# Attention and expert layers in eight tiles: two interleaved fronts and a third special step at the start

## The reference

```python
q, k = sigmoid(x Wq + bq), sigmoid(x Wk + bk); v = x Wv + bv
sink_in  = n / sum_d((q+e) * (cumsum(k)+e));  src_out = n / sum_d((k+e) * (cumsum(q)+e))
cons_sink = sum_d((q+e) * (cumsum(k*src_out)+e)) / n
cons_src  = exp(clip(sum_d((k+e) * (cumsum(q*sink_in)+e)) / n, -1, 1))
vs = v * cons_src / cumsum(cons_src) * n
a  = (q*sink_in/n) . cumsum(k outer vs) * sigmoid(cons_sink)
h  = layernorm(x + a Wo + bo); z = layernorm(h + gelu(h W1 + b1) W2 + b2)
x2 = layernorm(x + z)
y  = layernorm(x2 + sum_e gate_e * (relu(x2 wi + bi + x2 A_e B_e) wo + bo))
```

## Time and profile before

| what | us |
|---|---|
| median of 3 runs (lowest, highest) | 417.70 (417.43, 417.96) |
| the profiled execution's own time | 417.23 |
| its span, first to last instruction | 415.4 |
| busy: TensorE, VectorE, GpSimd, ScalarE | 374.7, 329.4, 252.0, 216.7 |
| mean granted clock of TensorE | 0.991 of full |

### The profile page before, as it was taken

The page is one execution under the profiler, slowest core; times in us unless marked ns, Lnnn a source line. Parts: engine busy times, 40 slices in busy tenths (PEclk is TensorE's granted clock), DMA queues, the critical chain, the costliest instruction groups (busy, mean ns, idle before and its releaser), DMA issues. The chain is left out here.

```text
span 415.4 us, 6622 instructions
## 1 busy us (share of the span) xinstructions
PE 374.7 (90%) x2082; PEld 261.7 (63%) x2082; DVE 329.4 (79%) x787; ACT 216.7 (52%) x399; POOL 252.0 (61%) x431
## 2 busy tenths in 40 slices
PE   8897799788998999989998999899999997799991
PEld 3555556475756875677657774778478755675551
DVE  3659966699599988999799979997899889732632
ACT  2240326327853586538852785279635864175441
POOL 2017245995289828975598449963898279836211
PEclk9999999899999999999999999999999999999997
DMA  8236006400180007300560028001800072000000
GB/s 260 113 75 154 1 2 156 123 2 0 39 216 2 0 2 188 93 0 0 122 158 2 1 71 211 2 0 29 211 17 0 2 178 51 0 1 28 14 13 25
DMA packets 19859, 26.59 MB, mean 64 GB/s; under 512 B 1648, under 2 KB 9968, under 8 KB 19824
## 3 DMA queue, kind: packets, MB, share of 16 engines
q1 hardware_dynamic: 19680, 25.96, 24.5%
q10 hardware_dynamic: 144, 0.21, 0.2%
HBM read 7.29 MB, written 2.10 MB: 23 GB/s over the span
## 5 line engine op out<-in xcount | busy, mean ns | idle before, releaser
L848 POOL TENSOR_TENSOR prod<-cum_kv,q_fac 128x512 f32<-128x512 f32 x64 | 92.3, 1452 | 31.6 <-DVE cum_kv L1054 24.7
L404 PEld LDWEIGHTS pO<-s_wor,prod 128*128 128x128 f32 x512 | 62.9, 193 | 34.1 <-POOL prod L848 21.5
L404 PE MATMUL pO<-s_wor,prod 128*128 128x128 f32 x512 | 70.3, 284 | 14.1 <-POOL prod L848 13.9
L1048 DVE TENSOR_TENSOR kv<-k,vb 128x512 f32<-128x512 f32 x64 | 52.9, 826 | 6.8 <-DMA vb<-vs 6.8
L835 POOL TENSOR_TENSOR var_eps<-mv,s_con 128x4 f32<-128x4 f32 x32 | 9.5, 296 | 59.4 <-DVE mv L1076 59.4
L1054 DVE TENSOR_TENSOR_SCAN cum_kv<-p_ones,cum_kv,kv 128x512 f32<-128x512 f32 x32 | 40.5, 1275 | 0.6
L1054 DVE TENSOR_TENSOR_SCAN cum_kv<-p_ones,kv 128x512 f32<-128x512 f32 x32 | 38.6, 1215 | 0.5
L657 ACT ACTIVATE v<-pA,s_att 128x512 f32<-128x512 f32 x7 | 4.8, 687 | 62.4 <-PE pA L340 62.4
L754 ACT ACTIVATE relu<-pG,s_att 128x512 f32<-128x512 f32 x28 | 19.1, 684 | 27.4 <-PE pG L490 27.4
L508 PEld LDWEIGHTS pY<-s_moe,gel 128*128 128x128 f32 x256 | 30.7, 192 | 3.7 <-issue 1.9
L508 PE MATMUL pY<-s_moe,gel 128*128 128x128 f32 x256 | 32.6, 277 | 0.0
(11 more groups left out here) (164 smaller groups left out, 806.2 us busy)
## 6 DMA issues: line engine op xcount, KB each, us to landing
vb<-vs SPq DMA_DIRECT2D x64, 256.0 KB, 4.6
xT<-x_t SPq DMA_DIRECT2D x8, 256.0 KB, 4.1
xt<-x SPq DMA_DIRECT2D x8, 256.0 KB, 5.1
out<-y SPq DMA_DIRECT2D x8, 256.0 KB, 2.3
s_moe<-moe_w SPq DMA_DIRECT2D x1, 836.0 KB, 10.1
s_wor<-wo_rep SPq DMA_DIRECT2D x1, 512.0 KB, 7.9
s_ffn<-ffn_w SPq DMA_DIRECT2D x1, 512.0 KB, 8.6
s_con<-consts SPq DMA_DIRECT2D x1, 502.0 KB, 4.5
```

Source lines behind the costliest of these rows:

```text
L404: mm = pe.matmul(pO3[:, s, :], prod[:, m % 4, s * P:(s + 1) * P], s_wor[:, m, :], start=False, stop=(m == DH - 1), skip_group_check=True)
L848: pool.tensor_tensor(prod[:, m % 4, :], cum_kv[t.par][:, m, :], q_fac[t.par][:, :], ALU.mult).then_inc(prod_ready, 1)
L1048: dve.tensor_tensor(kv[:, m % 3, :], k[t.par][:, :], vb[:, m, :], ALU.mult).then_inc(kv_ready, 1)
```

## The change

The step after the second gets a program of its own. Tile 1's q and k are projected in the opening, into two other banks (pG[1] and pM), and its first running sums and denominators are done there between those of tile 0. The second step keeps tile 0's outer products and the rest of tile 1's front, with no FFN; its VectorE program alternates running sums with other operations. The third step has tile 0's FFN and part of its experts, tile 1's outer products and FFN, and tile 2's front and first outer products. The general step starts at tile 2, and leaves out what the third step did for it. Several helpers get a further wait, since the buffers rden, rden_n, rden_x, kq, qk and vb are now written in another order. The diff, cut to its core (q_times_cum_k and the other sums get waits like those shown; head_sums and project_k follow the banks):

```diff
--- before
+++ after
+def q_bank(t):
+    return pG[1] if t.n == 1 else pA
+
+def k_bank(t):
+    return pM if t.n == 1 else pB
...
+def p_den(t):
+    return k_bank(t)[:, SUMS_AT:SUMS_AT + 2 * HW]
...
     def spread_vs(t, m):
         sp.wait_ge(vs_ready, t.n + 1)
+        wait(sp, kv_ready, DH * (t.n - 1) + m + 1)
...
+    load_xT(Tile(2))
...
     def project_q(t):
-        wait(pe, qfac_ready, t.n)
-        pe.matmul(pA[:, :], att("wq"), xT[t.par][:, :], start=True, stop=True).then_inc(q_proj, 1)
+        if t.n > 1:
+            pe.wait_ge(qfac_ready, t.n)
+        pe.matmul(q_bank(t)[:, :], att("wq"), xT[t.par][:, :], start=True, stop=True).then_inc(q_proj, 1)
...
     def project_v(t):
-        if t.n > 0:
+        if t.n == 1:
+            pe.wait_ge(qfac_ready, t.n)
+        elif t.n > 1:
...
     def denominators_T(t, i):
...
+            wait(pe, vs_ready, t.n)
...
@@ TensorE @@
     def opening(a):
+        b = a.plus(1)
         project_q(a); project_k(a); project_v(a)
-        keep_busy(1)
         pe.matmul(pO[:, :], onesrow[:, 0:P], onesrow[:, :], start=True, stop=True).then_inc(po_written, 1)
+        project_q(b); project_k(b)
         head_sums(a, 0, True); head_sums(a, 0, False)
         keep_busy(2)
         denominators_T(a, 0); denominators_T(a, 1)
         keep_busy(3)
         head_sums(a, 1, True); head_sums(a, 1, False)
         keep_busy(1)
+        head_sums(b, 0, True)
         cumulate_e(a)
-        keep_busy(2)
+        head_sums(b, 0, False)
+        keep_busy(1)
         compensation_T(a); factor_T(a)
+        keep_busy(3)
+        project_v(b)
+        denominators_T(b, 0); denominators_T(b, 1)
         constant_row()
-        project_q(a.plus(1)); project_k(a.plus(1))
-        keep_busy(4)
         pe.wait_ge(y_free[0], 16)
         reduce_out(a, 0)
     def second_step(b):
         a = b.plus(1)
-        keep_busy(2)
-        for m in range(1, 5):
-            reduce_out(b, m)
-        head_sums(a, 0, True); head_sums(a, 0, False); project_v(a)
         keep_busy(1)
-        reduce_out(b, 5)
-        denominators_T(a, 0); denominators_T(a, 1)
+        reduce_out(b, 1)
         keep_busy(1)
-        reduce_out(b, 6)
+        reduce_out(b, 2)
+        keep_busy(1)
         head_sums(a, 1, True)
         keep_busy(1)
         head_sums(a, 1, False)
         keep_busy(1)
+        reduce_out(b, 3)
+        keep_busy(1)
+        reduce_out(b, 4)
+        keep_busy(2)
+        reduce_out(b, 5)
+        cumulate_e(a)
+        keep_busy(1)
+        reduce_out(b, 6)
+        compensation_T(a); factor_T(a)
+        keep_busy(1)
         reduce_out(b, 7)
+    def third_step(c):
+        b, a = c.plus(1), c.plus(2)
+        project_q(a); project_k(a)
+        keep_busy(1)
+        project_v(a)
         keep_busy(2)
+        pe.wait_ge(y_free[1], 16)
+        h_T(c); hidden(c, 0); hidden(c, 1)
+        head_sums(a, 0, True); head_sums(a, 0, False)
+        hidden(c, 2); hidden(c, 3); ffn_out(c, 0)
+        reduce_out(b, 0)
+        ffn_out(c, 1)
+        reduce_out(b, 1)
+        ffn_out(c, 2)
+        denominators_T(a, 0); denominators_T(a, 1)
+        ffn_out(c, 3)
+        reduce_out(b, 2)
+        keep_busy(1, pM)
+        reduce_out(b, 3)
+        keep_busy(2, pM)
+        reduce_out(b, 4)
+        keep_busy(1, pM)
+        head_sums(a, 1, True)
+        keep_busy(1, pM)
+        head_sums(a, 1, False)
+        keep_busy(1, pM)
+        reduce_out(b, 5)
+        keep_busy(1, pM)
+        reduce_out(b, 6)
+        keep_busy(1, pM)
         cumulate_e(a)
-        keep_busy(2)
-        h_T(b); compensation_T(a); factor_T(a)
-        for f in range(FC):
-            hidden(b, f)
+        reduce_out(b, 7)
+        keep_busy(1, pM)
+        compensation_T(a); factor_T(a)
+        pe.wait_ge(cmoe_ready, 1)
+        x2_T(c)
+        keep_busy(1, pG[1])
+        logits(c)
+        h_T(b); hidden(b, 0); hidden(b, 1)
+        lora_in(c)
+        hidden(b, 2); hidden(b, 3)
         for f in range(FC):
             ffn_out(b, f)
-        keep_busy(3, pM)
+        u_T(c, True)
+        inter_base(c, 0); inter_base(c, 1)
+        u_T(c, False)
+        inter1(c, 0); inter1(c, 1)
         reduce_out(a, 0)
+        inter2(c, 0); inter2(c, 1)
...
     def step(s):
-        if s.n == 1:
-                    pe.wait_ge(y_free[1], 16)
-                    pe.wait_ge(cmoe_ready, 1)
...
-    run_steps(step, first=1, end=TILES)
+    third_step(Tile(0))
+    run_steps(step, first=2, end=TILES)
...
@@ ScalarE @@
     def spread_denominators(t, i):
+        wait(act, (facT_ready, compT_ready)[i], t.n)
...
-        q_out(a); k_out(a)
-        spread_denominators(a, 0); spread_denominators(a, 1); v_out(a)
+        b = a.plus(1)
+        q_out(a); k_out(a); v_out(a)
+        q_out(b); k_out(b)
+        spread_denominators(a, 0); spread_denominators(a, 1)
         source_exp(a); alloc_tanh(a); allocation(a)
         spread_scale(a, False); spread_scale(a, True)
-        q_out(a.plus(1)); k_out(a.plus(1))
         seed_x(a)
+        spread_denominators(b, 0); spread_denominators(b, 1); v_out(b)
     def second_step(b):
         a = b.plus(1)
-        v_out(a); spread_denominators(a, 0); spread_denominators(a, 1)
         source_exp(a); alloc_tanh(a); allocation(a)
-        normalise(b, 0)
         spread_scale(a, False); spread_scale(a, True)
-        h_out(b)
+    def third_step(c):
+        b, a = c.plus(1), c.plus(2)
+        q_out(a); k_out(a)
+        normalise(c, 0); v_out(a); seed_x(b); h_out(c)
+        gelu(c, 0); gelu(c, 1)
+        seed_h(c)
+        gelu(c, 2); gelu(c, 3)
+        spread_denominators(a, 0); spread_denominators(a, 1)
+        normalise(c, 1)
+        source_exp(a); alloc_tanh(a); allocation(a)
+        spread_scale(a, False); spread_scale(a, True)
+        normalise(c, 2)
+        x2T_out(c); normalise(b, 0); gate_exp(c); h_out(b)
         gelu(b, 0); gelu(b, 1)
-        seed_h(b)
-        gelu(b, 2); gelu(b, 3)
+        seed_h(b); gelu(b, 2); gelu(b, 3)
         seed_x(a)
+        u1T_out(c)
+        act.wait_ge(cmoe_ready, 1)
+        udT_out(c); relu(c, 0); relu(c, 1)
+        gated_constant(c)
         normalise(b, 1)
...
@@ GpSimd @@
     def second_step(b):
-        for m in range(1, DH):
+        for m in range(1, 4):
             product(b, m)
-        inverse_std(b, 0); e_normal(a); scaled_h(b); h_residual(b); attention_input(a)
-        shifted_x(b); inverse_std(b, 1); product(a, 0); scaled_n2(b)
+        attention_input(a)
+        for m in range(4, 6):
+            product(b, m)
+        e_normal(a)
+        product(b, 6); product(b, 7)
+    def third_step(c):
+        b, a = c.plus(1), c.plus(2)
+        inverse_std(c, 0); scaled_h(c); h_residual(c)
+        product(b, 0); product(b, 1); shifted_x(c); product(b, 2); product(b, 3)
+        attention_input(a)
+        product(b, 4); inverse_std(c, 1); scaled_n2(c)
+        product(b, 5); outer_residual(c)
+        product(b, 6); e_normal(a); product(b, 7); shifted_x(b)
+        inverse_std(c, 2); inverse_std(b, 0); scaled_h(b); h_residual(b)
+        product(a, 0); product(a, 1)
+        inverse_std(b, 1); product(a, 2); scaled_n2(b)
     def step(s):
-        if B: product(b, 1); product(b, 2)
+        if B and b.n > 2: product(b, 1); product(b, 2)
...
@@ VectorE @@
     def k_times_cum_q(t, pair):
+        wait(dve, (consp_ready, den_ready)[pair], 2 * (t.n + pair))
...
     def inverse_denominators(t):
+        wait(dve, qscale_ready, t.n)
...
     def normal_denominators(t):
+        wait(dve, rdenx_ready, 2 * t.n)
...
     def cumulate_sink(t):
+        if t.par == 1:
+            dve.wait_ge(cumqs_ready, t.n)
...
+    def opening(a):
+        b = a.plus(1)
+        cumulate_q(a); cumulate_k(a); k_times_cum_q(a, 0); q_times_cum_k(a, 0)
+        inverse_denominators(a); normal_denominators(a)
+        cumulate_q(b)
+        sink(a); cumulate_sink(a); source(a); k_times_cum_q(a, 1); cumulate_source(a); q_times_cum_k(a, 1)
+        cumulate_k(b)
+        k_times_cum_q(b, 0)
+        conserved(a); clip_source(a)
+        q_times_cum_k(b, 0)
+        prefix_e(a)
+        inverse_cum_e(a); source_factor(a); sink_factor(a)
+        inverse_denominators(b)
+        values(a); query_factor(a)
+        normal_denominators(b)
+        outer_product(a, 0); cumulate_kv(a, 0); outer_product(a, 1)
     def second_step(b):
         a = b.plus(1)
+        cumulate_kv(b, 1); outer_product(b, 2)
+        sink(a); cumulate_sink(a); k_times_cum_q(a, 1)
+        cumulate_kv(b, 2); outer_product(b, 3)
+        source(a); cumulate_source(a); q_times_cum_k(a, 1)
+        cumulate_kv(b, 3); outer_product(b, 4)
+        cumulate_kv(b, 4); outer_product(b, 5)
+        conserved(a); clip_source(a)
+        cumulate_kv(b, 5); outer_product(b, 6)
+        prefix_e(a)
+        cumulate_kv(b, 6); outer_product(b, 7)
+        inverse_cum_e(a); source_factor(a); sink_factor(a)
+        cumulate_kv(b, 7)
+        values(a); query_factor(a)
```

(51 more changed lines are left out.)

31 lines of the change are left out of this document (17 added, 14 removed).

## The result

In runs on one chip the changed kernel took 414.02 us in the median (413.77 to 416.07), the kernel before 417.70: ratio 0.9913 [0.9884, 0.9942]. It is faster by 3.7 us, 0.9%, where 6.0 us were forecast. A second set of runs of the same two kernels (experiment 9) gave 415.57 for 417.98, only 2.4 us, so the median gain is known to about 1 us. The profiled execution took 414.02 us with a span of 412.1, so 3.3 us less span than before.

What follows compares the result with a forecast made beforehand. A tile was taken as a 44.3 us loop between TensorE and VectorE with GpSimd, whichever arrives later setting the next tile; 6.4 us earlier less 0.4 for waits gave 6.0, 417.70 to 411.7 us, range 407.5 to 415.5.

Steps and rivals of the forecast that it cites:

- The wait before x2_T: Third step: TensorE waits 2.9 us for tile 0's late normalisation, then 1.2 GHz clock costs 1.7 us (bounds 0 to 2.2).
- TensorE's waits before the last reductions: Step 2: GpSimd is no longer late with its products, so 1.8 us of TensorE's idle time goes.
- Step 2 starts at 115.25: lead 3.85 us: Walk through second and third step: step 2's first matmul on TensorE comes at 115.25 instead of 119.09.
- the units: Durations from profile rows used for the walk, such as 0.60 us per VectorE 512-column operation, 1.48 per GpSimd product.
- Rival C: Second and third step: two-operand VectorE operations beside GpSimd products contend, gain shrinks by 3.5 to 2.5 us, 415.2; chance 0.14.
- case A: The forecast itself: 411.7 us, own range 409 to 414; chance 0.55.
- The alternation: VectorE, second and third step: running sums between other operations leave each GpSimd product a gap; no size given.
- Arrives 6.4 us early: TensorE at step 2's LoRA products: 3.85 + 1.8 + 0.7 us early, and the old loop runs 6.4 us earlier thereafter.
- A wait of over 2 us on VectorE before second_relu: Sign in the new trace: VectorE waits there over 2 us in tile 2 (of step 2) alone.
- rival B: VectorE's lead carries on, as the clock holds and TensorE drops more idle time: 8.7 us gain, 409.0; chance 0.20.
- the added waits: 39 further wait instructions on VectorE over tiles 3 to 7, likely hidden: 0.4 us, bounds 0 and 9.5.
- D: Rival: added waits exposed in tiles 3 to 7 at 0.243 us each, 9.5 us, giving 420.8; chance 0.11.

Runs made afterwards that it cites:

- experiment 9: The changed kernel run again with no edit, to see its spread, against the kernel before; 415.57 us, ratio 0.9935.
- after, operand in PSUM: Changed kernel with outer products leaving out factor k, multiplying vb with ones in PSUM, so one SBUF operand; 406.89 us, ratio 0.973.
- experiment 2: Changed kernel with three busy matmuls ahead of x2_T on TensorE in the third step, in place of idle time; 412.91 us, ratio 0.9891.
- experiment 12: Changed kernel with GpSimd's products 1 and 2 of tile 2 put back from the third step into step 2; 416.03 us, ratio 0.9952.
- experiments 10 and 11: Outer products without factor k, vb times ones in PSUM, in the changed kernel (406.89 us) and in the kernel before (407.77 us).
- experiment 6: Changed kernel with alternation undone in second and third step, outer products in twos and threes before their running sums; 416.58 us, ratio 0.9972.
- experiment 4: Kernel before with one swap in the general step, cumulate_kv(b, 3) in front of outer_product(b, 4); 417.91 us, ratio 1.0009.
- experiment 1: Changed kernel with moments(c, 2) moved ahead of the inverse of the exponentials on VectorE in the third step; 413.10 us, ratio 0.9887.

## Why the prediction was right, and where its size was off

The milestones (when an operation starts, or ends where that is said; us):

| | before | forecast | after | after, operand in PSUM |
|---|---|---|---|---|
| kv(0, 0) | 29.16 | 29.95 | 29.87 | 29.86 |
| values(1) | 63.18 | 53.7 | 54.39 | 53.55 |
| hidden(0, 0) | | 62.6 | 63.27 | 62.44 |
| sink(2) | | 72.95 | 73.70 | 72.86 |
| product 6 ends | | 86.9 | 88.69 | 86.74 |
| cumulate_e(2) inverted | | 89.3 | 91.20 | 89.26 |
| values(2) | | 91.6 | 93.50 | 91.95 |
| x2_T(0) | | 94.85 | 97.00 | 95.50 |
| hidden(1, 0) | 101.25 | 100.4 | 102.77 | 99.74 |
| step 2 | 119.09 | 115.25 | 118.39 | 114.93 |
| first sum of tile 3 | 133.36 | 124.7 | 128.16 | 124.23 |
| first sum of tile 7 | 310.43 | | 307.11 | 298.68 |

**Right.** The opening costs 0.71 us (0.8 forecast). The gain is made in the second step, and VectorE waits there for cumulate_e, though 1.01 us and not 2.5. The wait before x2_T is 3.02 us (2.9 forecast), with a stretch at 1.2 GHz behind it that costs 1.5 us by experiment 2 (1.7 forecast). TensorE's waits before the last reductions go: its lead grows from 0.70 to 2.9 us there, by 2.2 where I had 1.8. TensorE is what is late next. The loop keeps its 44.3 us a tile: (310.43 - 133.36) / 4 before, and (307.11 - 174.52) / 3 = 44.2 after.

From tile 3 on it looks otherwise: (307.11 - 128.16) / 4 = 44.7. This is over the 44.5 us that the prediction named as a sign of being wrong. The loop is not slower; the first of the four distances holds the 1.8 us that VectorE gives back in tile 3.

**Wrong size: the walk of the second and third step, "Step 2 starts at 115.25: lead 3.85 us".** The lead was 0.70. The 3.15 us are lost bit by bit: 0.75 by sink(2) (0.7 of it by values(1)), 1.0 from there to product 6, 0.4 to x2_T, 0.2 to hidden(1, 0), 0.8 to step 2. The term that failed is the units. I took them from rows in which nothing was slowed (kv 0.68, additions 1.69), for steps in which the change puts both engines' work with two SBUF operands side by side.

I had let contention drop because kv takes 0.68 us "in some places" and "both stand beside products". This reading was wrong. Beside the kv at 42.70 no product runs; GpSimd was idle from 40.70 to 44.72 (timeline of before, GpSimd):

```profile
39.44 1.26 POOL L848 TENSOR_TENSOR prod<-cum_kv,q_fac 128x512 f32<-128x512 f32 x1
44.72 1.26 POOL L848 TENSOR_TENSOR prod<-cum_kv,q_fac 128x512 f32<-128x512 f32 x1 [4.02 <-DVE cum_kv L1054]
```

And where a kv beside products kept 0.67 us, the products paid: 1.48 in a row of four, 1.27 with the operand in PSUM.

By the traces it was GpSimd's side that cost time. In the second step product 3 (1.63 us) and `attention_input` (2.16 for 1.65) make product 4 late, and reduction 4, reduction 5 and cumulate_e follow it: the 0.7 us. The kv of 1.45 and the e_pref of 1.35 us at 46.67 and 48.04 only used up VectorE's slack, since it still waited 1.01 us behind them. In the third step scaled_n2 and outer_residual take 2.29 and 2.14 us from start to start, each forecast at 1.65. That is 1.1 us, about the loss of 1.0 up to product 6. Of the last 0.8 us, 0.5 are `second`, which product 1 holds up: with this product moved away (experiment 12) u_T(0) and step 2 come 0.5 us earlier. The stall of `first` has not been taken away alone.

With the outer product's operand in PSUM the same order meets the forecast to 0.2 us up to cumulate_e(2). Some of that is luck: its products take 1.27 us where the walk has 1.48, and its e_pref still takes 1.00 and 1.27. Behind x2_T the comparison flatters me more: the clock did not fall in that execution. With the 1.5 us of experiment 2 added its step 2 would be at 116.4, so 2.0 of the 3.15 us go with the outer products' second SBUF operand and 1.2 don't. Of these 1.2, 0.65 are there at x2_T, 0.2 come by hidden(1, 0) and 0.3 in short pauses behind it. The gate's stalls are in that execution too (1.03 and 1.05 us) but cost it next to nothing, since TensorE waits less than 0.1 us before its u_T(0). Of the 0.65 us, 0.35 lie between cumulate_e(2) and moments(0, 2), which come at 90.65 for 90.3; the rest is in the chain behind and stays open.

So the size was wrong because the two sides were unlike: the measured time of before holds its contention, my walk of after did not. Rival C named the mechanism and put the loss at 3.5 us of the 6.0. The missing part was 2.3 us by the first set of runs and 3.6 by the second. My sum gave 6.0 with the likeliest case A, and the time came out at 414.0, between A and C: A's order of events, C's price in part. The Trainium skill (GPSIMD Engine Reference, Key points), cited for that rival, agrees with experiments 10 and 11: without the second SBUF operand outer products take 0.67 us and products 1.27.

**The alternation** brings its gain otherwise than the prediction had it: not by leaving GpSimd's products a gap, but by feeding them sooner (experiment 6). In the general step one such swap brought nothing (experiment 4).

**What survives.** "Arrives 6.4 us early" was 0.70 + 2.2 + 0.4 = 3.3 us. The last term, the short waits, I had at 0.7; two of the three are still there, 0.25 us at 138.68 and 0.24 at 144.99. "A wait of over 2 us on VectorE before second_relu" did not come: VectorE's lead of 5.2 us is given back earlier, above all at the head sums of tile 3 (1.43 us). How much is given back was right, as the bound by TensorE asks it (5.2 - 3.3 = 1.9); the place was wrong.

**Waits and rival B.** 0.4 us were forecast for the added waits and none were measured, so D is ruled out. B did not come either: experiment 1 kept the clock and took the idle time, and tile 7 followed step 2 (2.7 and 2.6 us), not VectorE's lead.

## What to carry to other kernels

When a new order sets two engines' work side by side, price it with the durations that such work has beside each other in the trace, or take the contention out of both sides of the comparison. Before a row is used as proof that two engines don't disturb each other, look whether the other engine was working at that moment. Put the small operation that feeds a long chain (here four moments) into a wait its engine has anyway, ahead of the operation that waits: in the traces it was worth 2.6 us here, of which 1.5 were TensorE's clock. Interleaving paid where it fed the downstream chain sooner; 39 more waits for something long past cost nothing that could be measured.
